# The product for B and C as four blocks of 128 tokens in four groups of output rows, and one product of B and u moved from GpSimd to VectorE

## What is computed

```python
xn = rmsnorm(layernorm(x)); xs, res = split(xn @ W_in)      # 512 channels each
xs = silu(causal_conv(xs) + conv_b)
dt, B, C = split(xs @ W_x)                                   # 512, 16 and 16 columns
dt = softplus(dt @ W_dt)                                     # W_x's first part times W_dt is made once
h = exp(A * dt) * h + (dt * xs) * B;  y = sum_n(h * C)       # over the tokens, 512 channels x 16 states
x = x + (y * silu(res)) @ W_out
x = x + (silu(xn2 @ w1[e]) * (xn2 @ w3[e])) @ w2[e]          # expert e has tokens 512 e to 512 e + 511
```

## Time and profile before

| | before |
|---|---|
| median of 3 runs | 986.62 us (986.61 to 986.76) |
| the profiled execution | 985.27 us |
| its span, first to last instruction | 983.5 us |
| mean granted clock of TensorE | 0.983 |
| busy: PE, DVE, POOL, ACT | 913.5, 900.4, 892.1, 732.3 us |

### The profile page before, as it was taken

How to read it: one execution, slowest core, us unless ns; L and a number is a source line. 1 busy time by engine, 2 the same in 40 slices (tenths; PEclk the granted TensorE clock), 3 DMA queues, 4 the chain that set the end, 5 groups by cost and what they waited for, 6 DMA issues and landing times.

```text
span 983.5 us, 13018 instructions
## 1 busy us (share of the span) xinstructions
PE 913.5 (93%) x4172; PEld 594.7 (60%) x4172; DVE 900.4 (92%) x966; ACT 732.3 (74%) x1305; POOL 892.1 (91%) x425
## 2 busy tenths in 40 slices
PE   6989989999999999999999999999999998769898
PEld 4545455655765576755856566754766556745765
DVE  5889899899999999999999999999999989999951
ACT  4667877978778878888779877888788785567630
POOL 1498899999999999999999999999999999999920
PEclk9999999999999999999999999999999999779899
DMA  5580154012642049021651038120580027200110
GB/s 175 222 298 22 43 215 173 29 40 100 260 157 67 1 171 343 4 68 59 233 225 43 25 103 340 76 68 12 190 315 21 27 95 277 102 22 3 59 50 21
DMA packets 43476, 116.82 MB, mean 119 GB/s; under 512 B 8592, under 2 KB 27024, under 8 KB 34192
## 3 DMA queue, kind: packets, MB, share of 16 engines
q1 hardware_dynamic: 41552, 115.94, 32.2%
q10 hardware_dynamic: 1856, 0.04, 0.1%
HBM read 110.21 MB, written 5.77 MB: 118 GB/s over the span
## 4 chain that ended last, share of the span: by engine, by line
PE 36%; DVE 36%; ACT 15%; issue 11%; DMA 1%; POOL 0%; DVEq 0%; SPq 0%; ACTq 0%; POOLq 0%
DVE ring L658 25%; PE gbank L1091 19%; DVE ring L643 9%; PE ybank L1154 7%; PE gbank L1105 6%; ACT ebank L787 4%; ACT hb L1020 2%; ACT sres L868 1%; ACT xs L864 1%; ACT L1016 1%; PE gbank L1099 1%; ACT L876 1%; ACT L872 1%; DMA hb<-in_L_attn_W_x_dram 1%; PE gbank L1225 1%
## 5 line engine op out<-in xcount | busy, mean ns | idle before, releaser
L658 DVE TENSOR_TENSOR_SCAN ring<-ebank,state,ring 128x512 f32<-128x512 f32 x512 | 623.7, 1267 | 28.8 <-ACT ebank L787 21.6
L516 POOL TENSOR_TENSOR hc<-ring,c_all 128x1024 f32<-128x1024 f32 x255 | 600.8, 2381 | 14.0 <-DVE ring L658 6.4
L787 ACT ACTIVATE ebank<-dt_,a_neg 128x512 f32<-128x512 f32 x512 | 347.2, 689 | 165.0 <-DVE ring L658 162.5
L1154 PEld LDWEIGHTS ybank<-ident,hc 128*128 128x128 f32 x2048 | 237.8, 144 | 106.5 <-issue 52.0
L1154 PE MATMUL ybank<-ident,hc 128*128 128x128 f32 x2048 | 265.2, 278 | 31.9 <-POOL hc L516 23.2
L502 POOL TENSOR_TENSOR ring<-b_all,u 128x1024 f32<-128x1024 f32 x109 | 259.5, 2381 | 9.9 <-DVE taken L607 9.5
L643 DVE TENSOR_TENSOR ring<-b_all,ubank 128x1024 f32<-128x1024 f32 x145 | 173.4, 1196 | 0.0
L1091 PE MATMUL gbank<-xT,w 128*128 128x512 f32 x320 | 148.1, 597 | 15.2 <-DVE hb L738 12.4
L1091 PE MATMUL gbank<-xT,w_a 128*128 128x512 f32 x256 | 119.1, 602 | 8.3 <-DVE dt_ L632 4.4
L1091 PEld LDWEIGHTS gbank<-xT,w 128*128 128x128 f32 x320 | 57.3, 190 | 82.2 <-issue 56.7
L1091 PE MATMUL gbank<-xs,w_a 128*128 128x512 f32 x224 | 100.8, 593 | 0.7 <-ACT sres L805 0.7
(11 more groups left out here) (146 smaller groups left out, 750.9 us busy)
## 6 DMA issues: line engine op xcount, KB each, us to landing
b_all<-bc_kept SPq DMA_DIRECT2D x32, 1024.0 KB, 6.7
c_all<-bc_kept SPq DMA_DIRECT2D x32, 1024.0 KB, 8.4
w<-in_L_ffn_w_dram SPq DMA_DIRECT2D x16, 640.0 KB, 4.9
w_a<-in_L_attn_W_in_dram SPq DMA_DIRECT2D x7, 1024.0 KB, 4.9
w_a<-wc_kept SPq DMA_DIRECT2D x7, 1024.0 KB, 4.8
w2s<-in_L_ffn_w_dram SPq DMA_DIRECT2D x8, 640.0 KB, 9.4
xin<-in_L_attn_x_dram SPq DMA_DIRECT2D x9, 512.0 KB, 3.6
x<-in_L_attn_x_dram SPq DMA_DIRECT2D x7, 512.0 KB, 6.4
```

The source lines that it names most:

```text
L516: ch_ok.by(e.tensor_tensor(hc[:, q % HC, :, :], ring[:, q % RING, :, :], c_all[:, n:n + NG, :], ALU.mult))
L658: h_ok.by(e.tensor_tensor_scan(row, ebank[j % 2][:, :], row, initial=state[:, q, n:n + 1], op0=ALU.mult, op1=ALU.add))
L787: e_ok.by(e.activation(ebank[j % 2][:, :], dt_[:, d, :], ACT.Exp, scale=a_neg[:, d, k:k + 1]))
L1154: last = e.matmul(ybank[:, cols(b)], hc[:, q % HC, n, cols(b)], ident[:, :], is_transpose=True, start=(k == 0 and n == 0 and b == 0), stop ...
```

## The change

From chunk 1 on (the product made in iteration 0 is the first of its form) each of the four blocks of 128 tokens gets a matmul of its own, with its output in rows 32 b to 32 b + 31 of the bank, for each of the four blocks of channels: 16 matmuls of 128 columns. ScalarE copies 128 x 128 into the first quarter of `yt` in place of 32 x 512 into `hb`. It waits for the turning of y that stands last before it (YT 0, or YT 1 in iteration 0); the next copy of y into `yt` waits for the store. The store puts the blocks in order again. Tile 21 leaves `POOL_BU`, in chunks 1 to 7; so GpSimd has 13 and VectorE 19 products.

```diff
@@ -31,7 +31,7 @@
-    POOL_BU = (1, 4, 7, 10, 11, 14, 17, 18, 21, 22, 23, 24, 27, 29)
+    POOL_BU = (1, 4, 7, 10, 11, 14, 17, 18, 22, 23, 24, 27, 29)
@@ -69,6 +69,8 @@
         bc_s = hb[0:W, FT, :]
+        bc_b = yt[:, 0:P]
+        BC_AFTER = (1, 0)
@@ -414,7 +416,7 @@
-                    e.dma_start(bc_kept[:, :], bc_s).then_inc(bc_out.sem, 16)
+                    e.dma_start(bc_kept[:, :].rearrange("m (b t) -> b m t", b=NT), bc_b).then_inc(bc_out.sem, 16)
@@ -883,14 +885,19 @@
             def bc_read(c, i):
-                bc_out.wait(e, c - 1)
                 bank = wait_full(e, i, "BC", 0)
-                read_out(e.activation(bc_s, bank[0:W, :], ACT.Copy), i, "BC", 0)
+                if c == 0:
+                    read_out(e.activation(bc_s, bank[0:W, :], ACT.Copy), i, "BC", 0)
+                else:
+                    wait_full(e, i, "YT", BC_AFTER[i > 0])
+                    read_out(e.activation(bc_b, bank[:, 0:P], ACT.Copy), i, "BC", 0)
 
             def y_read(d):
                 def job(c, i):
 
                     y_ok.wait(e, c, GPD * (d + 1))
+                    if has_front(i) and d == BC_AFTER[i > 0] + 1:
+                        bc_out.wait(e, c + 1)
@@ -1267,7 +1274,11 @@
                 bank = wait_free(e, i, "BC", 0)
-                filled(product(bank[0:W, :], [(wbc[:, k, :], xs[:, k, :]) for k in range(ND)]), i, "BC", 0)
+                for k in range(ND):
+                    for b in range(NT):
+                        last = e.matmul(bank[b * W:(b + 1) * W, 0:P], wbc[:, k, :], xs[:, k, cols(b)], start=(k == 0), stop=(k == ND - 1),
+                                        skip_group_check=True)
+                filled(last, i, "BC", 0)
```

## The result

The changed kernel takes 992.49 us, median of 4 runs (991.17 to 994.83), against 986.62 us before (986.12 to 986.76): 1.0063 times as long, 95% interval 1.0051 to 1.0075. It is slower by 5.9 us where I had written 987.3 us and a range up to 992.0. The 992.6 us of rival (d) lie nearest to the measured time, but by luck: its mechanism did not happen. The profiled execution took 992.72 us, its span is 990.6 us; before it was 983.5 us. The traces are thus 7.1 us apart, more than the medians, since the profiled execution of before (985.27 us) was 1.35 us faster than its kernel's median.

The account below looks back on a forecast made before the run. Each chunk was taken as bound by a stretch of VectorE, one of ScalarE and 37 us of TensorE, not GpSimd. Terms +1.5 - 0.8 = +0.7 us on the 986.6 us median gave 987.3 us, range 985.0 to 992.0.

Parts of the forecast that it names:

- rival (d): TensorE's transposes after the B and C product: they don't keep the clock up, falls in six chunks, 992.6 us; chance 0.03.
- I cost the edit at nothing, and the cover is that wait.: B and C product: its saving only lengthens TensorE's wait for GpSimd's C product, 0.4 to 2.2 us; no net change.
- rival (a): TensorE's two lengthened idle times per chunk: the clock falls and the kernel gets slower, 991.0 us; chance 0.35.
- Of eleven places: TensorE's lengthened waits: two to four clock falls, about 1.2 us each on average, +3.7 us taken.
- The product takes 1.8 us: B and C product on TensorE: 1.8 us in place of 3.6 a chunk, bounds 0.9 and 3.7.
- Rival (c): B and C product on TensorE: the groups do not overlap, it takes 3.7 us, total 987.3 us; chance 0.08.
- Tile 21 delays the hidden product by 0.5, TensorE by 0.3: VectorE's new product after scan 20: +0.3 us a chunk in chunks 1 to 5, +1.5 us in all.
- GpSimd hands nothing on in chunks 1 to 6: GpSimd without tile 21's product: gets 2.3 us of idle time a chunk, no gain, since its C product waits for VectorE's scan.
- rival (b): GpSimd, busy 112.3 of 113.2 us, is the real pace: less work there makes it faster, 979.2 us; chance 0.14.
- The last chunk gives 0.8: Last chunk, where GpSimd is behind: one product less removes VectorE's and TensorE's waits for it, -0.8 us, bounds 0 and -0.9.

Follow-up runs that it names:

- e7: Kernel before plus the B and C edit alone, its product issued three times over in iteration 0, once from iteration 1 on: 987.37 us, ratio 1.0011.
- e3: Changed kernel with the 32 passes of the product for B and C issued three times over: 990.27 us, ratio 1.0042.
- e1: Kernel before plus the B and C edit alone, tile 21 left on GpSimd: 990.83 us, ratio 1.0044.
- e5: Kernel before with tile 21 on VectorE from chunk 1 on, its product made behind the hidden products: 989.04 us, ratio 1.0030.
- e9: Kernel before with tile 21 moved to VectorE, ahead of the hidden products, and the first term of UP 1 issued once more: 987.51 us, ratio 1.0007.
- e4: Kernel before with tile 21 on VectorE in the last chunk alone: 984.41 us, ratio 0.9982.
- e6: Changed kernel with the product for B and C three times over and the first term of UP 1 issued once more: 987.05 us, ratio 1.0008.
- e2: Kernel before with tile 21 moved to VectorE alone, B and C made and stored as before: 989.99 us, ratio 1.0040.
- e10: Kernel before with tile 21 on VectorE in the last chunk alone and, in iteration 0, RES 2's first term four times more: 983.69 us, ratio 0.9976.
- e11: Kernel before with tiles 21 and 23 on VectorE in the last chunk alone: 985.74 us, ratio 0.9993.

## Why the prediction was wrong, step by step

- **"I cost the edit at nothing, and the cover is that wait."** This is the step that failed. As waiting it holds: e7's undisturbed chunks are 113.17 us, and no wait for the store appears. ScalarE's copy waits for YT 1 in iteration 0, 0.7 us in e7 and 2.36 in the profile of the change (I had written under 1), but its next exponential waits for VectorE's scan even so. The copy takes 0.28 us in place of 0.57. But the cover was itself worth something. TensorE's work that nobody waits for kept its clock up, and where it became idle time the work behind could run at 1.2 GHz: 5.29 us for the 8 passes of DT 0 in iteration 0, and 3.67 with the product three times over (e3). I had this as rival (a), and gave it 0.35 where the sum got 0.40.
- **"Of eleven places" in rival (a).** They were all taken from chunk 4. The B and C product also stands in iteration 0, in another order: its wait was 0.69 us there and became 3.21. By e1 against e7 that place costs 3.5 us (3.3 in the profile of the change), the largest single term of the result. In chunks 1 to 6 the forecast of (a), 2 to 4 falls at 1.2 on average, is about right: two, at 1.17 and 1.69 us in the profile of the change; one to three in e1 to e3. One at the transposes costs 1.1 rather than 0.8, one at the hidden product 1.7 as written.
- **The product takes 1.8 us.** It takes 1.08, near the lower bound of 0.9: the four groups overlap almost wholly. The reason given for taking twice the bound does not hold: 32 passes in four groups are 8 one behind the other, so a quarter of 3.7 us already has the two passes of one matmul in series. Rival (c) is out. The Trainium skill's 2.38 for three groups (TensorE: Matmul & The Clock Gate, Packing small matmuls) gave 1.5; measured against 3.7 us for 32 passes in series the four reach 3.4 times.
- **Tile 21 delays the hidden product by 0.5, TensorE by 0.3.** Right to the rows: 0.48, less the 0.19 of slack; 113.45 instead of 113.18 us. e9, with the delay and without falls, is within 0.1% of before.
- **GpSimd hands nothing on in chunks 1 to 6.** Right; rival (b) is out. GpSimd lost 2.3 us a chunk, and e5 and e9, which also take them away, have no shorter chunk.
- **The last chunk gives 0.8.** It gave 2.0 (e4). I took one wait, at 914.72, for all that GpSimd's lag costs. The lag also made GpSimd's last product run beside VectorE's at L692 (0.65 us) and lengthened TensorE's wait at the end (0.3).
- **Rival (d), transposes.** Out: in the changed kernel TensorE did only transposes and waits from 427.19 to 434.62 us, and likewise between 541.74 and 548.47; the clock fell in the first and held in the second. It fell in one of six such chunks, where (d) wanted it in each. Before the change the clock even rose in such a stretch: from 867.73 us on TensorE did nothing but transposes, and the clock went from 0.50 (872 to 874) over 0.71 (874 to 876) to 1.00 (876 to 878). The Trainium skill says that transposes do not count in the same way (TensorE: Matmul & The Clock Gate, PE-mode transpose); this rise disagrees with it. The row with the wait before that stretch, in TensorE's timeline before:

```profile
867.73 1.97 PE L1154 MATMUL ybank<-ident,hc 128*128 128x128 f32 x8 [5.34 <-ACT yt L898]
```

Put together from the profile of the change, without the 1.3 us of its start: delay 0.5 at the first hidden product and 5 x 0.27 = 1.3 behind it, last two chunks -2.1, falls 1.6 + 1.7 + 1.2 + 1.7 = +6.2, in sum +5.9, as by the medians. The 6.2 agree with the 6.0 us that e6 takes away. What stays open is why a fall takes one chunk and not another with the same waits, and how the short product at 114 us brings about the low stretches at 140 and 153. That the two profiles of the change agree on the chunks, and that e2's falls stand in every second chunk (341.87, 570.48, 799.22), suggests that it is no pure chance, but no run tests it.

## What to carry to other kernels

Before an engine's work is made smaller where nothing waits for it, look at what follows: if it is TensorE and it then waits, price the work behind the wait at the low clock, since here 2.5 us saved in each chunk made falls that cost 3.3 us in iteration 0 and 1.2 in one of six later chunks, and repeated work in their place took the loss away. Price an edit at every place where it stands, the first and the last iteration among them, and not at the periodic chunk alone. Move work off an engine only in the chunk where it is late: tile 21 in the last chunk alone gave 2 us (e4); in all chunks from 1 on it cost 3.5 (e2).

## What the runs showed of the hardware that I had not expected

- A wait of 1.79 us before the hidden product let the clock fall in none of the chunks 1 to 6 of the profiles of before, e1, e4, e5, e7, e10 and e11; one of 2.27 us let it fall in three of these six chunks in e2, in two in e3 and in one in each profile of the change. Half a microsecond of idle time, or one repeated term of 0.86 us, decided over 1.7 us.
- The wait alone does not tell whether the clock falls: behind 2.17 us it stayed up before the change (136.43) and fell in the change (139.30).
- Two waits of 1.24 and 1.23 us with 1.06 us of transposes between them (430.69 to 432.99) also let it fall, in one of six chunks, in the profiles of the change, e1 and e7 alike.
- VectorE's 128 x 512 product of two SBUF operands took 1.34 us where GpSimd's last product lay beside it for 0.8 us (before, 940.67), and 0.69 where it lay beside it for 0.1 (e4, 940.73); VectorE's scans (2.46 us a pair) and its products with an operand in PSUM (1.20) kept their time beside GpSimd (before, 917 to 940 us).
